# A three-layer relational graph network on one core: gathers without a fill between them, and the first layer's dense pieces planned over its gathers

## The chip, the core and the metric

The kernel runs on one core of a Trainium2 chip. The core has five engines that run side by side, each through its own queue in order, and that meet only at semaphores: TensorE (PE in the profile, its weight loads PEld), VectorE (DVE), ScalarE (ACT), GpSimd (POOL) and SyncE (SP). Sixteen DMA engines move data between HBM and the on-chip memory SBUF; matmuls write into PSUM. What counts is the device time of one execution in microseconds, lower is better.

## What is computed

```python
def _rgcn_conv(x, edge_index, edge_type, W, root, bias):
    src, dst = (edge_index[0], edge_index[1])
    x_src = x[src]
    out = x @ root + bias
    for r in range(N_REL):                       # 4 relations
        mask = (edge_type == r).astype(x.dtype)
        s = segment_sum(x_src * mask[:, None], dst, num_segments=N_NODES)
        c = segment_sum(mask, dst, num_segments=N_NODES)
        mean = s / jnp.maximum(c, 1.0)[:, None]
        out = out + mean @ W[r]
    return out
...
h = x                                            # 6250 x 128, float32
for l in range(2):
    h = relu(_rgcn_conv(h, ..., weights[l], roots[l], biases[l]))
h = _rgcn_conv(h, ..., weights[2], roots[2], biases[2])
return _layernorm(x + h)
```

There are 6250 nodes of 128 features, 100,000 edges sorted by destination and 3 layers. The destinations are drawn as the square of a uniform number, so the first nodes have many incoming edges and the last ones few.

## The kernel before, in words

Edges stand in tiles of 128, 782 of them, and four tiles make a group (196 groups, the last one with two tiles, of which the last has 32 edges). A layer treats them in two ways.

**Sparse groups.** The groups from a certain one on are gathered: the table `ytab` in HBM holds, for each node and relation, the row h @ W[r] (512 bytes), GpSimd issues an indirect DMA for each tile (L734, `gather`) that fetches 128 rows into one quarter of a slot of `ring`, VectorE builds for each tile a 128x128 selection matrix `S` (L1358), and TensorE adds rows times `S` into one of the banks `psGR` and `psRB` (L899), from where VectorE adds a group to the node's columns (`node`, L1380). The first layer gathers 138 groups (550 tiles), the other two 119 groups (474 tiles) each, 1498 tiles in all. The ring has nine slots of four tiles, so GpSimd may be up to 36 tiles ahead of TensorE; then it waits on `s_pe`. Gathers of a layer can start only when the last rows of `ytab` for it have landed.

**Dense windows.** The groups of the first nodes, which have many edges each, are not gathered. They are put together into windows of at most 116 nodes, 5 windows in the first layer and 9 in the others. Of each a count matrix over all 6250 source nodes is built, in 49 blocks: binned records (items "P" and "N": VectorE L1389 to L1393, TensorE L950 and L952), then one-hot matrices on VectorE (L1408, L1409), their product on TensorE (L997), a copy by ScalarE (L1081), and the product with the layer's own rows (L981). A piece of two blocks is a "C" item, 25 pieces a window. Windows built in a layer are kept in HBM (`a_dram`), the next layers load them (`aring`, L1057). The first layer builds windows 0 to 4, the second loads these and builds 5 to 8, the third loads all nine. When a window is whole, the items "M", "F" and "G" scale its sum and multiply it by the weights (L924), the result being added like a group.

**Ends.** As soon as all edges of a block of 128 nodes are in, an "E" item applies the relu and makes the block's rows for the next layer (L775, L780, L781, ScalarE L1010), which SyncE stores to `ytab`. The last layer has "L" items with the layer normalization in their place. The first window's nodes end last, after all dense windows ("late" blocks 0 to 4 in the first layer).

**The order.** All of this stands in one list of items for each layer, and every engine runs its part of that list in order. The list is made by `schedule`, a planner that simulates the layer with costs written out by hand. It assumes that a gather takes `GATHER` = 1.36 us in the first layer and 1.25 us in the others, and it gives each dense item a due time, `due`, that moves by `pace` times the item's cost. A sparse group goes first when the planner believes that it has arrived; a dense item goes in when it is due. With `pace` at 1.0 dense items stand as early as their costs allow; above 1.0 they are spread over the gathers until `ENDING` = 100 us ahead of the last gather:

```python
pace = max(1.0, (sum(ntile) * gather - ENDING) / sum(max(cost(li, it)) for it in dense)) if li else 1.0
```

so that in the first layer it is 1.0 whatever the sums are. The planner's own start times for that layer are `START_POOL` = 95 us and `START_PE` = 205 us.

**The fill.** Behind every gather GpSimd runs `rest` (L724): a memset of 160 int32 on one partition of a tile that nobody reads, `pause`. It waits for the memset before it and nobody else waits for it.

Ahead of all this the kernel turns the input arrays into tiles, makes the first layer's `ytab` (until about 99 us) and counts edges for the scales, on VectorE until about 200 us; the fast path starts on TensorE at 219 us.

Of the kernel before, what the change touches and what calls it, by code (L numbers as in the profile page):

```python
# [8 lines left out]
I32 = mybir.dt.int32  # L9
# [11 lines left out]
NL = 3  # L21
RW = 1024
FAR = 1000000
PAUSE = 160
EPS = 1e-5
WINDOWS = (5, 9, 9)
SPAN = 116
# [2 lines left out]
LAG, ENDING, BEHIND, SPREAD, TURN = 12.0, 100.0, 20.0, 10.0, 6.0  # L30
# [79 lines left out]
def schedule(pl, R):  # L110
# [11 lines left out]
    def cost(li, it):  # L122

        if it[0] == "X":
            return 0.0, 0.7, 0.7
        if it[0] == "P":
            c = pl.win[it[1]][2]
            return 4 * (0.12 + c * 0.04), 1.1 + 4 * (0.07 + 2 * c * pl.NB / 960), 0.0
        if it[0] == "C":
            c, m = pl.win[it[1]][2], len(pl.pieces[it[2]])  # L130
            if it[1] in pl.built[li]:
                return m * (0.44 + 0.22 * c), 0.44 * m * c, 1.0 * m
            return m * 0.44, 0.0, 0.4 * m
        return {"N": (0.0, 2.0, 0.0), "M": (0.5, 0.0, 0.6), "F": (0.0, 0.7, 0.0), "G": (0.9, 0.6, 0.0)}[it[0]]

    for li in range(NL):
        W, KH, sparse = pl.W[li], pl.KH[li], pl.sparse[li]
        NS = len(sparse)
        ntile = [min(4, pl.NT - 4 * g) for g in sparse]
        gather = GATHER[li > 0]  # L140
        start = START_PE if li == 0 else 0.0
        pe = dve = act = start
        pool = START_POOL if li == 0 else 0.0
        arrive, eaten, items = [], [], []
        dense = []
# [22 lines left out]
                        dense.append(("N", w + 1))  # L168
            dense.append(("F", w))
        dense.append(("G", W - 1))  # L170
        pace = max(1.0, (sum(ntile) * gather - ENDING) / sum(max(cost(li, it)) for it in dense)) if li else 1.0
        due = start
        done, late = KH, list(range(KH))
        batch, batches, added = [], [], [0, 0]
# [99 lines left out]
def rgcn_kernel(nc, x, src, dst, typ, weights, roots, biases, c_ident, c_iota, c_tri, c_col, c_need,  # L274
# [30 lines left out]
    rows_of = [min(P, E - t * P) for t in range(NT)]  # L305
    width = [c * NB for _, _, c in pl.win]
    layers = schedule(pl, R)


# [73 lines left out]
    with ctx:  # L383
        sb = lambda name, shape, dt=F32: ctx.enter_context(nc.sbuf_tensor(name, shape, dt))
# [26 lines left out]
        flagf = sb("flagf", [1, 2])  # L411
        brow = sb("brow", [1, 2, NP], I32)
        idxc = sb("idxc", [P, NT4], I32)
        pause = sb("pause", [1, PAUSE], I32)
        relc, wc = sb("relc", [P, NT4]), sb("wc", [P, NT4])
        vals = sb("vals", [P, TH, 2], F16)
        colc = sb("colc", [P, TH])
# [66 lines left out]
        rest = room + NB * P - (2 * NB * P + AF * PIECE * NR * P + AS * CH * NR * P // 2)  # L484
        if rest > 0:
# [9 lines left out]
        tbank = lambda u: (psT + psY)[u % TB]  # L495
        banks_of = lambda li, w: psC[pl.second[li][w]]

        names = ("s_e0 s_e1 s_e2 s_k0 s_k1 s_c s_x0 s_x1 s_w0 s_w1 s_fill s_rest s_idx s_dst s_tot s_prod s_end s_car s_aw s_vio "
                 "s_tp s_tev s_fl s_small s_sm s_st s_xt s_pb s_pu "
                 "s_ym s_rm s_yev s_rev s_tA s_tV s_S s_pe s_acc s_fin s_sq s_sd s_no s_v2 s_v3 "  # L500
                 "s_bd s_oh s_dn s_fd s_fp s_bc s_mb s_xa s_cv tSP tPE tACT tDVE tPOOL gd gp s_xw s_n1").split()
        q = {n: sem(n) for n in names}
# [213 lines left out]
            ring_need[n] = ring_total[n % R]  # L716
        AHEAD = min(R, sbase[1])

        rests = [0]

        def rest(e):
            if rests[0]:
                e.wait_ge(q["s_rest"], rests[0])
            e.memset(pause[:], 0).then_inc(q["s_rest"], 1)  # L724
            rests[0] += 1

        def gather(e, n):
            li, g = sgroups[n]
            if n >= R:
                e.wait_ge(q["s_pe"], n - R + 1)  # L730
            for i, t in enumerate(tiles[g]):
                m = rows_of[t]
                at = (n % R) * 512 + i * P
                e.indirect_dma_start(ring[0:m, at:at + P], None, Y[li % 2],  # L734
                                     bass.IndirectOffsetOnAxis(ap=idxc[0:m, t:t + 1], axis=0)
                                     ).then_inc(s_ring[n % R], 16)
                rest(e)

        def gpsimd_engine(e):
            tail = FULL // 32 * 32  # L740
            e.memset(U[tail:NP, 0:RW].bitcast(I32), 0)
            e.memset(U[tail:NP, RX:RX + RW].bitcast(I32), 0)
            last = e.memset(a_dstx[tail:NP, :], FAR)
            if tail:
                last = e.memset(a_dstx[0:1, 0:1], -1)
            last.then_inc(q["s_fill"], 1)
            e.wait_ge(q["s_tev"], 1)
            y_stored(e, 0)
            for n in range(AHEAD):
                gather(e, n)  # L750
            branch(e, "POOL", pool_fast)

        def pool_fast(e):
            for n in range(AHEAD, NN):
                if n in sbase:
                    y_stored(e, sgroups[n][0])
                gather(e, n)
# [951 lines left out]
```

## Time and profile before

| | us |
|---|---|
| median of 3 runs | 2343.55 |
| lowest, highest | 2343.26, 2344.71 |
| the profiled execution | 2337.83 |
| its span in the trace | 2335.9 |

The span of the trace is 1.9 us shorter than the profiled execution's own time, and that is 5.7 us below the median of the runs. The profile names engines as above; a line number is a line of the kernel before. "Busy" is time in which an instruction of the engine runs, an idle time is put down to what ended it, and "issue" means that nothing in the trace explains it. PEclk is the clock that TensorE was granted, as a share of full speed. Where several forms or buffers share a line they are one group.

In the profiled execution the first layer's gathers start at 99.5 us, the second's at 1000.1 us, the third's at about 1668 us, and the last gather at 2314.5 us.

### The profile page before, as it was taken

The numbers are of one execution on the slowest core, as the hardware profiler recorded it, in microseconds if no ns is written. First come the engines' busy times: TensorE is split into PE (matmuls) and PEld (weight loads), VectorE is DVE, ScalarE is ACT, GpSimd is POOL, SyncE is SP. The second block draws the span as 40 slices with busy tenths as digits, with TensorE's granted clock in tenths as the row PEclk, the third lists the DMA queues.
The fourth block names the chain that finished last, engine by engine and source line by source line (L and its number), as shares of the span: only waits on it lengthen the run. The fifth ranks groups of instructions, "written<-read, shape, count | busy, mean of one in ns | idle before, by whom it ended". The sixth has DMA issues, their size and how long they took to land.

```text
span 2335.9 us, 29108 instructions
## 1 busy us (share of the span) xinstructions
PE 1622.7 (69%) x7831; PEld 1152.8 (49%) x7831; DVE 1249.9 (54%) x4096; ACT 1003.1 (43%) x1499; POOL 1893.7 (81%) x3004
## 2 busy tenths in 40 slices
PE   6513667878998854559898778776577677777643
PEld 4312334545665543347675545544355566665532
DVE  4988889988887522223277665552133233333342
ACT  4300002455788710156666556662344444444200
POOL 0293998888888888678888888888488888888885
PEclk9756667999999965779999899997689888888855
DMA  6300222333444432377654344444455555555321
GB/s 202 125 27 23 60 63 86 106 106 124 140 166 160 167 106 66 95 229 218 218 180 146 124 133 139 139 155 128 148 187 154 165 177 168 170 176 173 106 82 47
DMA packets 164859, 314.38 MB, mean 135 GB/s; under 512 B 34816, under 2 KB 85120, under 8 KB 164692
## 3 DMA queue, kind: packets, MB, share of 16 engines
q1 hardware_dynamic: 113096, 210.74, 26.3%
q0 software_dynamic: 47936, 98.12, 14.9%
q10 hardware_dynamic: 3660, 3.60, 0.6%
q8 instruction: 67, 1.10, 0.2%
q14 instruction: 100, 0.82, 0.1%
HBM read 206.52 MB, written 105.80 MB: 134 GB/s over the span
## 4 chain that ended last, share of the span: by engine, by line
POOL 65%; issue 11%; PE 9%; DVE 8%; DMA 4%; ACT 1%; ACTq 1%; DVEq 0%; SPq 0%; POOLq 0%
POOL ring L734 52%; POOL pause L724 13%; DMA aring<-a_dram 3%; PE psD L981 2%; PE psY L775 2%; ACT afull L1057 1%; DVE rows L1208 1%; PE psRB L899 1%; DVE V L1409 1%; DMA ring<-ytab,idxc 1%; DVE V L1408 1%; ACTq L1027 1%; PE psT L775 1%; DVE S L1358 1%; PE psRB L781 0%
## 5 line engine op out<-in xcount | busy, mean ns | idle before, releaser
L734 POOL DMA_INDIRECT ring<-ytab,idxc x1498 | 1526.5, 1019 | 421.2 <-issue 241.4
L981 PE MATMUL psD<-afull,xs 128*128 128x512 f32 (+1 forms) x1666 | 579.4, 476 | 60.7 <-ACT afull L1057 33.2
L1358 DVE TENSOR_SCALAR S<-iota,relc,wc 128x128 f32<-128x128 f32 x1498 | 426.9, 371 | 161.9 <-PE psGR L899 91.4
L1057 ACT ACTIVATE afull<-aring 128x1024 fp32r<-128x1024 f16 (+1 forms) x350 | 346.7, 1033 | 240.4 <-DMA aring<-a_dram 133.0
L899 PE MATMUL psRB<-S,ring 128*128 128x128 f32 x1516 | 254.7, 321 | 228.1 <-DMA ring<-ytab,idxc 220.0
L899 PE MATMUL psGR<-S,ring 128*128 128x128 f32 x1480 | 249.8, 323 | 219.2 <-DMA ring<-ytab,idxc 208.0
L981 PEld LDWEIGHTS psD<-afull,xs 128*128 128x128 f32 (+1 forms) x1666 | 336.0, 209 | 133.5 <-issue 32.5
L724 POOL MEMSET pause<- 1x160 int32 x1498 | 370.1, 247 | 0.1
L899 PEld LDWEIGHTS psRB<-S,ring 128*128 128x128 f32 x1516 | 227.2, 226 | 269.5 <-issue 210.7
L899 PEld LDWEIGHTS psGR<-S,ring 128*128 128x128 f32 x1480 | 225.5, 229 | 258.0 <-issue 210.2
L1085 ACT ACTIVATE aring<-afull 128x1024 f16<-128x1024 f32 (+1 forms) x225 | 234.0, 1040 | 21.0 <-ACT afull L1081 0.7
L1408 DVE TENSOR_SCALAR V<-iota,recs 128x128 f16<-128x128 f16 x588 | 163.8, 279 | 121.6 <-PE psT L997 73.6
L1081 ACT ACTIVATE afull<-psT 128x512 fp32r<-128x512 f32 x299 | 173.8, 593 | 123.5 <-PE psT L997 121.2
L1409 DVE TENSOR_SCALAR V<-iota,recs 128x512 f16<-128x512 f16 x588 | 212.3, 361 | 0.0
L981 PE MATMUL psB<-afull,xs 128*128 128x512 f32 (+1 forms) x588 | 167.1, 431 | 6.2 <-ACT afull L1057 6.0
L997 PE MATMUL psT<-V 128*128 128x512 f16 x394 | 146.2, 408 | 6.0 <-DVE V L1409 5.7
L1380 DVE TENSOR_TENSOR node<-node,psRB 128x128 f32 x199 | 57.3, 288 | 161.6 <-issue 75.3
L1064 ACT ACTIVATE xs<-xst 128x512 fp32r<-128x512 f32 (+1 forms) x39 | 23.2, 595 | 271.2 <-DMA xst<-in_x 248.8
L981 PEld LDWEIGHTS psB<-afull,xs 128*128 128x128 f32 (+1 forms) x588 | 115.0, 206 | 33.5 <-ACT afull L1057 8.6
L1380 DVE TENSOR_TENSOR node<-node,psGR 128x128 f32 x200 | 57.6, 288 | 135.0 <-DVE node L1380 64.7
L1010 ACT ACTIVATE yst<-psT 128x512 f32<-128x512 f32 (+1 forms) x62 | 36.8, 594 | 213.3 <-PE psT L775 213.3
L1081 ACT ACTIVATE afull<-psY 128x512 fp32r<-128x512 f32 x142 | 84.1, 592 | 70.4 <-PE psY L997 69.8
(198 smaller groups left out, 1569.4 us busy)
## 6 DMA issues: line engine op xcount, KB each, us to landing
aring<-a_dram SPq DMA_DIRECT2D x168, 512.0 KB
a_dram<-aring SPq DMA_DIRECT2D x108, 512.0 KB
ytab<-yst SPq DMA_DIRECT2D x144, 256.0 KB
ring<-ytab,idxc POOLq DMA_INDIRECT x1498
hrows<-yst SPq DMA_DIRECT2D x96, 64.0 KB
xst<-hrows SPq DMA_DIRECT2D x24, 256.0 KB
xst<-in_x SPq DMA_DIRECT2D x12, 256.0 KB
yst<-in_x SPq DMA_DIRECT2D x11, 256.0 KB, 4.3
```

Of the source, the lines that this page charges most:

```text
L724: e.memset(pause[:], 0).then_inc(q["s_rest"], 1)
L734: e.indirect_dma_start(ring[0:m, at:at + P], None, Y[li % 2], bass.IndirectOffsetOnAxis(ap=idxc[0:m, t:t + 1], axis=0)).then_inc(s_ring[n ...
L899: last = e.matmul(o, ring[0:m, at:at + P], S[0:m, n % NS, i, :], start=(i == 0), stop=(i == len(tiles[g]) - 1))
L981: last = e.matmul(bank[:], xs[0:m, s, i, :], a, start=(i == 0 and s == 0), stop=(i == NB - 1 and s == 1))
L997: e.matmul(tbank(u)[:], ohs[:, v % NO, :], ohk[:, v % NO, :], start=(j == 0), stop=(j == c - 1)).then_inc(q["s_bd"], 1)
L1057: e.activation(afull[:, n % AF, 0:m, :], aring[:, cc % AS, o:o + m, :], ACT.Copy).then_inc(q["s_cv"], 1)
L1081: e.activation(afull[:, n % AF, j, :], tbank(u)[:], ACT.Copy).then_inc(q["s_tA"], 1)
L1085: e.activation(aring[:, cc % AS, half:half + m, :], afull[:, n % AF, 0:m, :], ACT.Copy).then_inc(q["s_cv"], 1)
L1358: last = e.tensor_scalar(S[:, n % NS, i, :], iota[:], relc[:, t:t + 1], wc[:, t:t + 1], ALU.is_equal, ALU.mult)
L1380: e.tensor_tensor(w, w, part[bank][:, j * P:(j + 1) * P], ALU.add).then_inc(q["s_acc"], 1)
L1408: e.tensor_scalar(ohs[:, v % NO, :], iota16[:, 0:P], recs[:, 0, at:at + 1], None, ALU.is_equal)
L1409: e.tensor_scalar(ohk[:, v % NO, :], iota16[:], recs[:, 1, at:at + 1], None, ALU.is_equal).then_inc(q["s_oh"], 1)
```

## The change

It has two parts. The fill behind every gather goes, with its tile, its constant and its semaphore. And `pace` is worked out for the first layer as for the others, from the time between the planner's start of the dense work and its last gather: for that layer it becomes (95 + 550 x 1.36 - 205 - 100) / 420.2 = 538 / 420.2 = 1.28, with 420.2 us the sum of its dense costs. For the other layers `pool` and `start` are zero, the value is what it was, and their lists of items are the same item for item. `GATHER` is left as it is.

```diff
-PAUSE = 160
...
-        pace = max(1.0, (sum(ntile) * gather - ENDING) / sum(max(cost(li, it)) for it in dense)) if li else 1.0
+        pace = max(1.0, (pool + sum(ntile) * gather - start - ENDING) / sum(max(cost(li, it)) for it in dense))
...
-        pause = sb("pause", [1, PAUSE], I32)
...
-        rests = [0]
-
-        def rest(e):
-            if rests[0]:
-                e.wait_ge(q["s_rest"], rests[0])
-            e.memset(pause[:], 0).then_inc(q["s_rest"], 1)
-            rests[0] += 1
-
         def gather(e, n):
...
                                      ).then_inc(s_ring[n % R], 16)
-                rest(e)
```

On GpSimd, where the fast path begins (behind the branch on `flag_i`), before:

```order
L706 TENSOR_LOAD flag_i
L706 ISA x2
L707 COMPARE_AND_BRANCH
L734 DMA ring<-ytab,idxc 128x128
L724 MEMSET pause 1x160
L734 DMA ring<-ytab,idxc 128x128
L724 MEMSET pause 1x160
```

and after, with all the rest of the three layers' gathers:

```order
L704 TENSOR_LOAD flag_i
L704 ISA x2
L705 COMPARE_AND_BRANCH
L724 DMA ring<-ytab,idxc 128x128 x513
L724 DMA ring<-ytab,idxc 32x128
L724 DMA ring<-ytab,idxc 128x128 x473
L724 DMA ring<-ytab,idxc 32x128
```

A gather is now followed at once by the next one; nothing else stands between them but, at each fourth, the wait on `s_pe` for a free slot.

On TensorE, at the end of the first layer's last dense window (`psD<-afull,xs` is the product of a block, `psRB<-V,wt` the window's "G", `x4` of `S,ring` one group, and `psT` or `psY<-wt,node` the first of the three matmuls of an "E"), before:

```order
L899 MATMUL psGR<-S,ring 128x128 x4
L997 MATMUL psY<-V 128x512
L981 MATMUL psD<-afull,xs 128x512 x2
L997 MATMUL psT<-V 128x512
L981 MATMUL psD<-afull,xs 128x512 x2
L997 MATMUL psT<-V 128x512
L981 MATMUL psD<-afull,xs 128x512 x6
L924 MATMUL psRB<-V,wt 128x128 x4
L775 MATMUL psY<-wt,node 128x512
L780 MATMUL psY<-ident,node 128x128
L781 MATMUL psY<-node,rt 128x128
L899 MATMUL psRB<-S,ring 128x128 x12
```

and after:

```order
L986 MATMUL psT<-V 128x512
L970 MATMUL psD<-afull,xs 128x512 x2
L888 MATMUL psRB<-S,ring 128x128 x4
L986 MATMUL psY<-V 128x512
L970 MATMUL psD<-afull,xs 128x512 x6
L913 MATMUL psRB<-V,wt 128x128 x4
L888 MATMUL psRB<-S,ring 128x128 x8
L888 MATMUL psGR<-S,ring 128x128 x8
```

The rows look alike, but they stand at another place among the groups: the last dense piece stands behind 104 of the 138 groups before and behind 113 after. Up to the 52nd group the two lists are the same; from there on the dense items move back little by little, by 9 groups at the end. The blocks 0 to 4 ("late") move from behind the 109th group to behind the 117th, and the other ends from the 111th group on keep about the place that they had.

## Rows read from the trace of the kernel before

**Rows 1.** The page: the chain that ended last, shares of the span.

```profile
POOL 65%; issue 11%; PE 9%; DVE 8%; DMA 4%; ACT 1%; ACTq 1%; DVEq 0%; SPq 0%; POOLq 0%
```

**Rows 2.** GpSimd's groups: line, engine, operation, xcount | busy us, mean ns | idle before.

```profile
L734 POOL DMA_INDIRECT ring<-ytab,idxc x1498 | 1526.5, 1019 | 421.2 <-issue 241.4 <-DMA ytab<-yst 95.9 <-DMA hrows<-yst 45.4
L724 POOL MEMSET pause<- 1x160 int32 x1498 | 370.1, 247 | 0.1
```

**Rows 3.** Timeline of GpSimd: start us, us, engine line operation [idle before].

```profile
979.86 0.22 POOL L724 MEMSET pause<- 1x160 int32 x1
1000.11 0.96 POOL L734 DMA_INDIRECT ring<-ytab,idxc  x1 [20.03 <-DMA hrows<-yst]
...
120.54 0.66 POOL L724 MEMSET pause<- 1x160 int32 x1
121.36 1.99 POOL L734 DMA_INDIRECT ring<-ytab,idxc  x1 [0.16 <-issue]
```

**Rows 4.** Busy us (x) by stretch: PE, PEld, DVE, ACT, POOL, then clock, DMA, GB/s.

```profile
219.00:400.00 181.00, 127.58 (x572) 77.03 (x572) 158.78 (x449) 22.85 (x38) 161.68 (x212) 0.70 0.23 67
400.00:800.00 400.00, 349.08 (x1773) 225.10 (x1774) 334.12 (x1283) 268.11 (x413) 355.36 (x550) 0.94 0.41 138
800.00:1000.00 200.00, 103.98 (x427) 74.52 (x426) 52.55 (x199) 32.51 (x85) 158.44 (x268) 0.68 0.32 98
1000.00:1200.00 200.00, 169.09 (x855) 132.76 (x856) 70.69 (x226) 130.55 (x148) 176.07 (x295) 0.95 0.70 221
1200.00:1668.00 468.00, 348.78 (x1714) 234.14 (x1712) 256.73 (x967) 261.76 (x443) 398.34 (x654) 0.90 0.40 134
1668.00:2336.00 668.00, 435.91 (x2023) 354.70 (x2023) 214.27 (x786) 237.62 (x262) 561.99 (x948) 0.79 0.48 149
```

**Rows 5.** By stretch, the fills (L724) alone: busy us (x), clock, DMA, GB/s.

```profile
400.00:800.00 400.00, 77.28 (x275) 0.94 0.41 138
800.00:1000.00 200.00, 31.20 (x134) 0.68 0.32 98
...
1200.00:1668.00 468.00, 82.12 (x327) 0.90 0.40 134
1668.00:2336.00 668.00, 110.50 (x474) 0.79 0.48 149
```

**Rows 6.** TensorE's waits (us, times, longest), in 400:800, 800:1000, 1200:1668, 1668:2336.

```profile
PE psGR L899 <- DMA ring<-ytab,idxc: 6.5, 3, 3.1
PE psRB L899 <- DMA ring<-ytab,idxc: 2.6, 5, 0.9
...
PE psRB L899 <- DMA ring<-ytab,idxc: 43.8, 15, 4.4
PE psGR L899 <- DMA ring<-ytab,idxc: 39.0, 11, 4.3
...
PE psRB L899 <- DMA ring<-ytab,idxc: 52.9, 30, 4.0
PE psGR L899 <- DMA ring<-ytab,idxc: 52.7, 27, 4.2
...
PE psRB L899 <- DMA ring<-ytab,idxc: 102.8, 44, 4.6
PE psGR L899 <- DMA ring<-ytab,idxc: 91.5, 40, 5.2
```

**Rows 7.** Timeline of TensorE: one group behind the first layer's dense work.

```profile
855.06 2.04 PE L899 MATMUL psRB<-S,ring 128*128 128x128 f32 x8 [3.44 <-DMA ring<-ytab,idxc]
```

**Rows 8.** The chain that ended last: the last gather, from its start to landing.

```profile
2314.46 2.13 DMA ring<-ytab,idxc
```

**Rows 9.** Timeline of GpSimd and VectorE beside each other.

```profile
504.39 0.95 POOL L734 DMA_INDIRECT ring<-ytab,idxc  x1 [0.16 <-issue]
504.57 0.24 DVE L1408 TENSOR_SCALAR V<-iota,recs 128x128 f16<-128x128 f16 x1
504.73 0.34 DVE L1409 TENSOR_SCALAR V<-iota,recs 128x512 f16<-128x512 f16 x1
```

More of the change, by code:

```diff
@@ L496, in rgcn_kernel @@
         banks_of = lambda li, w: psC[pl.second[li][w]]
-        names = ("s_e0 s_e1 s_e2 s_k0 s_k1 s_c s_x0 s_x1 s_w0 s_w1 s_fill s_rest s_idx s_dst s_tot s_prod s_end s_car s_aw s_vio "
+        names = ("s_e0 s_e1 s_e2 s_k0 s_k1 s_c s_x0 s_x1 s_w0 s_w1 s_fill s_idx s_dst s_tot s_prod s_end s_car s_aw s_vio "
                  "s_tp s_tev s_fl s_small s_sm s_st s_xt s_pb s_pu "
```

## The prediction

> **What bounds the kernel now.** Read first the chain that ended last: GpSimd holds 65% of the span and unexplained issue time 11% [rows 1]. Then GpSimd's groups: 1498 gathers of 1019 ns on average and as many fills of 247 ns; of the idle time ahead of gathers 241.4 us is "issue", some 0.16 us each [rows 2]. A quiet cycle is thus 0.95 (gather) + 0.22 (fill) + 0.16 (gap) = 1.33 us. Over a layer it is more, since VectorE holds GpSimd up now and then: 1.41 us a tile in the third layer (668 us for 474), 1.54 in the first from 219 us on (781 us with both ends, 515 tiles).
>
> Then the busy times by stretch [rows 4], beside TensorE's waits for gathers [rows 6]; they show where a faster gather would be felt. From 219 to 400 us VectorE is busy for 158.8 of 181 us. From 400 to 800 TensorE (349 of 400) and VectorE (334) are both near full, and TensorE waits 9 us for gathers. From 800 to 1000 the dense work is over, and TensorE waits 82.8 us. From 1000 to 1200 the second layer loads windows (221 GB/s), and there no wait of TensorE for a gather stands in the view. From 1200 to 1668 these waits are 105.6 us, in the third layer 194.3 us. So gathers bound three stretches of six.
>
> **Part 1, the fill goes: what a cycle becomes.** The trace has no gather that follows directly on another. Lower bound: the span of the gather itself, 0.95 us. Upper bound: 1.33 us, because a gather after 20.03 us of idle takes 0.96 us and the one 0.38 us behind its predecessor takes 0.95, and because the gap behind a fill is 0.16 us even where the fill took 0.66 us [rows 3]. If a gather left hidden work behind it of more than 0.38 us, the short break would show it, and a long fill would shorten the gap. Less than 0.38 us of such work can't be seen. I take 1.11 us, gather and gap without the fill: the gap is always there ahead of a gather and is nearest to a cost of starting one.
>
> The Trainium skill ("Perfetto Trace Analysis", on GpSimd's profiler boundary) says that GpSimd's spans don't compose and that such instructions are to be timed from start to start. What agrees here is only that the sole spacing in the rows is 1.33 us; by that rule 0.95 us is no lower bound, and the saving of a removed fill is anything between nothing and more than its length.
>
> **Where it is felt.** In a stretch the gain is the smaller of what the fills cost there [rows 5] and what TensorE waits [rows 6].
>
> First layer. 219 to 400: 106 fills of 0.247 = 26 us, but VectorE has only 181 - 159 = 22 us to spare: 15. 400 to 800: 77 us of fills against 9 us of waits: 9. The other 68 us are not lost: GpSimd runs ahead until the ring of 36 tiles is full. At the stretch's end it is some 6 ahead now (a landing of 2.13 us [rows 8] and a group of four), so 30 more, worth 30 x 1.11 = 33 us. 800 to 1000: 31 us of fills + 33 of lead = 64 of the 82.8 us of waits. Together 88 us.
>
> Second layer. 1000 to 1200: no waits, no gain, but a fuller ring; VectorE and the loads set the pace there, and GpSimd is ahead already, so I count 25 of its 36 us (147 fills of 0.247). 1200 to 1668: 82 + 25 = 107 us against 105.6 of waits. The two don't meet piece by piece, and I take 90.
>
> Third layer. Fills 110.5 us against 194.3 us of waits, nothing else late: the loads are 149 GB/s where the second layer had 221 with TensorE 169 of 200 us busy. I take 102, since locks that fell on a fill (247 - 220 = 27 ns a tile, 13 us) partly fall on the gather instead.
>
> **Part 2, the first layer's order.** The last dense piece stands behind 104 groups before, behind 113 after. Nothing is added: the same items in another order, with SyncE's stores and VectorE's one-hots along with them. A group costs TensorE 2.04 us [rows 7]. Nine groups, 18 us of TensorE's work, come out of the stretch in which it idles and go into the one in which it is full, and the 36 tiles they hold are then eaten before the gather-bound stretch starts. Without part 1 this is worth nothing: the layer ends with its last gather either way. With part 1 the last stretch has 98 tiles, of which 30 are in the ring: 68 x 1.11 = 75 us of gathers instead of 36 more tiles, 115 us; against the 18 us put ahead that leaves at most 22 us, of which TensorE's own work (200 - 82.8 - 18 = 99 us there, some 25 of it the end of the layer) allows little. The blocks 0 to 4 end behind group 117 of 138, still under cover. I take 7 us; the bounds are 0 and 22.
>
> **Sum.** 88 + 7 + 90 + 102 = 287 us. 2337.8 - 287 = 2051; with the 5.7 us by which the median lies above the profiled execution, about 2056 us. The setup up to 219 us is VectorE's and stays: the 36 fills in it stand ahead of a full ring.
>
> **The rivals.** First, the gap goes too, because a gather is taken up while another runs: 1.00 us a cycle. Another 0.11 x 474 = 52 us in the third layer, where 92 us of waits are left; 8 more in the second, where few are left; 15 in the first. About 1980 us. For it: the fill starts at the gather's end without a gap. Against it: the gap stands ahead of every gather, whatever came before. 12%.
>
> Second, a gather leaves hidden work of 0.2 to 0.35 us, which the fill covered; the cycle is about 1.25 us (the planner's own number for the later layers). Saved are 0.08 a tile against a quiet cycle, some 0.10 with the locks on fills gone: 47 us in each later layer, 50 in the first. 2343.5 - 145 = about 2200 us. Nothing in the rows speaks against it. 20%.
>
> Third, all 0.38 us are dead time and the fill was free: no change, 2343 us. The rows would allow it only if the dead time were just as long as fill and gap; and the new order alone gives nothing. 5%.
>
> Fourth, the slower end: without an instruction between them each gather is held until its predecessor's transfer has moved on. Its landing is 2.13 us behind its start [rows 8], so this could cost anything from 0 to 0.8 us a tile; it decides from a cycle of 1.33 us on. At 1.50 us it costs 0.15 x 948 = 142 us in the later layers and about 15 in the first: 2500 us. Against it: now the next gather starts 1.33 us behind the last, well before that landing, unhindered. 6%.
>
> A fifth one, slower too: gathers in a row shut VectorE out, and the breaks of 0.38 us are where it gets in. Full exclusion would make a layer the sum of both engines' work: in the first layer 545 us of VectorE [rows 4] and about 541 of gathers in 781 us. That sum, 1086, is larger than the stretch, and one-hots start and end inside a gather [rows 9]. So only short parts of a gather exclude. Over the three layers gathers and gaps at 1.11 us for 1462 tiles are 1623 us and VectorE's work 1087 us [rows 4], against some 2050 us in which they are gathered now; it takes an exclusion of 40% of VectorE's time to be slower, and half of it gives +120 us, about 2460. Today's cycle in the first layer, at most 0.2 us a tile above the quiet one with 1.06 us of VectorE beside each, allows 20%. 3%.
>
> The Trainium skill ("SBUF — State Buffer", on the shared port pair) states this rule: either side holds the pair "for the full instruction". The trace doesn't agree (two one-hots of 0.24 and 0.34 us within a gather of 0.95); by the rule, with all 1087 us excluded, the time would be near 3000 us.
>
> **Chances.** The forecast of 2056 us: 54%, for itself between 2000 and 2120. The first rival 12%, second 20%, third 5%, fourth 6%, fifth 3%. The range of 8 in 10 takes in the forecast's own, most of the second rival and half of the first: 1975 to 2240. A measurement of this kernel tells 0.2%, about 5 us, from no change. Faster 0.86, the same 0.05, slower 0.09.
>
> **What would show it.** In the new timeline gathers of 0.95 us start 1.11 us apart: 1.00, 1.25 or 1.33 name the first, second or third rival, longer gathers the fourth, longer one-hots and `S` builds the fifth. Waits of GpSimd on TensorE for a free slot should come up between 600 and 800 us and near 1200 us, and nowhere in the third layer. TensorE's waits for gathers should be some 20 us in the first layer's tail, under 20 in the second layer, near 90 in the third. The layers should be shorter by 95, 90 and 102 us. The forecast is wrong if the spacing is not 1.11 us, or if dense work turns out to be late where gathers were: then the third layer's gain is smaller than 100 us with waits for gathers gone.

## The result, and the profile after

| | median us | runs | kernel before beside it |
|---|---|---|---|
| first comparison | 2217.38 | 4 (2216.14 to 2218.82) | 2343.41 (4 runs) |
| once more, in the last set of runs | 2216.65 | 2 | 2345.52 (3 runs) |

The ratio is 0.9462, 95% interval 0.9445 to 0.9478; the second time 0.9455 (0.9427 to 0.9483). The change takes 126 us off, 5.4%. The forecast was 2056 us, a gain of 287 us, so less than half of the expected gain came; the time is near that of the second rival (2200 us) and inside the range. The profiled execution took 2218.8 us, its span is 2217.0 us. Between the two traces the difference is 118.9 us, since the profiled execution of the kernel before lies 5.7 us below its median and that of the changed kernel 1.4 us above. The chain that ended last (as in [rows 1]) is still GpSimd's first of all:

```profile
POOL 49%; issue 18%; DVE 15%; PE 9%; DMA 5%; ACT 1%; DVEq 1%; ACTq 1%; SPq 0%; POOLq 0%
```

What a gather costs now stands in the timeline of GpSimd (as in [rows 3]: start, us, engine, line, operation, idle before):

```profile
1106.35 0.94 POOL L724 DMA_INDIRECT ring<-ytab,idxc  x1 [0.30 <-issue]
1107.60 0.95 POOL L724 DMA_INDIRECT ring<-ytab,idxc  x1 [0.30 <-issue]
```

and in its group (as in [rows 2]):

```profile
L724 POOL DMA_INDIRECT ring<-ytab,idxc x1498 | 1553.1, 1037 | 639.5 <-issue 449.0 <-DMA ytab<-yst 95.4 <-DMA hrows<-yst 48.5
```

The fill's 0.22 us are gone, but the gap ahead of a gather has grown from 0.16 to 0.30 us: undisturbed gathers start 1.25 us apart (1106.35 and 1107.60), where it was 1.33. That is 0.08 us, not 0.22. "Issue" went from 241.4 to 449.0 us, which eats 208 of the 370 us that the fills had. And the gather itself is 1037 ns on average instead of 1019 (18 ns a tile, 27 us). VectorE is what lengthens both. In the trace of before, of the full-size gathers behind 225 us the 448 beside which VectorE ran nothing took at most 0.96 us, and those beside which it was busy up to 2.57 us; a fill took 221 ns without VectorE beside it and 266 with it. In the changed kernel 431 gathers had no VectorE beside them, again at most 0.96 us. So the time that fills had lost to VectorE (some 37 us in all) falls on the gathers in good part.

The stretches (as in [rows 4]: PE, PEld, DVE, ACT, POOL, then clock, DMA share, GB/s). The layers' gathers now start at 99.0, 964.4 and 1601.7 us, the last one at 2195.4:

```profile
400.00:800.00 400.00, 342.32 (x1741) 223.40 (x1740) 327.88 (x1272) 256.30 (x395) 311.45 (x291) 0.93 0.41 136
800.00:966.00 166.00, 100.02 (x426) 69.31 (x424) 49.17 (x190) 43.33 (x100) 108.36 (x114) 0.72 0.37 118
966.00:1166.00 200.00, 170.87 (x857) 135.22 (x858) 70.38 (x227) 130.99 (x148) 152.43 (x157) 0.95 0.72 225
1166.00:1589.00 423.00, 337.15 (x1699) 228.00 (x1697) 253.48 (x966) 256.98 (x433) 314.24 (x317) 0.91 0.44 143
1589.00:2217.00 628.00, 419.00 (x2038) 339.40 (x2036) 211.95 (x786) 240.28 (x272) 450.42 (x474) 0.83 0.52 160
```

The third layer of the kernel before starts at 1676.7 us, and not at about 1668, which lies in the wait ahead of it. The row in its timeline is

```profile
1676.69 0.96 POOL L734 DMA_INDIRECT ring<-ytab,idxc  x1 [25.41 <-DMA hrows<-yst]
```

The second layer's gathers now start 35.7 us earlier (964.4 for 1000.1), the second layer is 39 us shorter (637 for 677), the third 44 (615 for 659). That is 0.07, 0.08 and 0.09 us for each of the 514, 474 and 474 tiles: gathers still set the pace in all three. TensorE's waits for them (as in [rows 6]) say so too; in 800:966, 1166:1589 and 1589:2217:

```profile
PE psRB L888 <- DMA ring<-ytab,idxc: 26.4, 11, 3.8
PE psGR L888 <- DMA ring<-ytab,idxc: 25.0, 8, 3.8
...
PE psGR L888 <- DMA ring<-ytab,idxc: 38.2, 26, 3.7
PE psRB L888 <- DMA ring<-ytab,idxc: 37.9, 25, 3.7
...
PE psRB L888 <- DMA ring<-ytab,idxc: 84.8, 45, 3.5
PE psGR L888 <- DMA ring<-ytab,idxc: 75.9, 41, 4.8
```

51 us where it was 82.8, 76 where it was 105.6, 161 where it was 194.3. GpSimd waited for a free slot only at the start, as before (the longest in each row of `psGR` below is that one; the others are within the 0.30 us that stand ahead of every gather), so the ring was never full later. The first row is of the kernel before:

```profile
POOL ring L734 <- PE psGR L899: 37.6, 3, 37.3
...
POOL ring L724 <- issue: 449.0, 1473, 0.3
POOL ring L724 <- PE psGR L888: 42.5, 8, 40.3
POOL ring L724 <- PE psRB L888: 4.3, 14, 0.3
```

### The profile page after: what moved, and what is told of

It is laid out like the page before. It is cut to its first block, busy times and chain, and to the rows that moved or that the text cites. A ratio compares the mean times of both kernels' runs of the same rounds, so it can differ in the third digit from the quotient of the medians.

```text
span 2217.0 us, 27610 instructions
## 1 busy us (share of the span) xinstructions
PE 1591.0 (72%) x7831; PEld 1130.9 (51%) x7831; DVE 1239.0 (56%) x4096; ACT 1002.8 (45%) x1499; POOL 1556.1 (70%) x1506
## 4 chain that ended last, share of the span: by engine, by line
POOL 49%; issue 18%; DVE 15%; PE 9%; DMA 5%; ACT 1%; DVEq 1%; ACTq 1%; SPq 0%; POOLq 0%
POOL ring L724 49%; DMA aring<-a_dram 2%; PE psY L764 2%; DVE V L1398 2%; DVE S L1347 2%; DMA ring<-ytab,idxc 2%; DVE V L1397 2%; DVE V L1382 1%; PE psD L970 1%; DVE rows L1197 1%; PE psT L764 1%; PE psRB L888 1%; DVEq L1355 1%; ACT afull L1046 1%; DVE node L1369 1%
## 5 line engine op out<-in xcount | busy, mean ns | idle before, releaser
L724 POOL DMA_INDIRECT ring<-ytab,idxc x1498 | 1553.1, 1037 | 639.5 <-issue 449.0
L970 PE MATMUL psD<-afull,xs 128*128 128x512 f32 (+1 forms) x1666 | 572.8, 472 | 59.6 <-ACT afull L1046 33.1
L1347 DVE TENSOR_SCALAR S<-iota,relc,wc 128x128 f32<-128x128 f32 x1498 | 418.4, 365 | 114.5 <-PE psGR L888 74.3
L888 PE MATMUL psRB<-S,ring 128*128 128x128 f32 x1516 | 246.3, 313 | 178.6 <-DMA ring<-ytab,idxc 171.4
L888 PE MATMUL psGR<-S,ring 128*128 128x128 f32 x1480 | 241.6, 316 | 175.5 <-DMA ring<-ytab,idxc 158.1
L888 PEld LDWEIGHTS psRB<-S,ring 128*128 128x128 f32 x1516 | 220.7, 220 | 219.2 <-issue 178.0
L888 PEld LDWEIGHTS psGR<-S,ring 128*128 128x128 f32 x1480 | 218.6, 223 | 213.7 <-issue 167.8
L970 PE MATMUL psB<-afull,xs 128*128 128x512 f32 (+1 forms) x588 | 159.2, 416 | 6.0 <-ACT afull L1046 6.0
L999 ACT ACTIVATE yst<-psT 128x512 f32<-128x512 f32 x66 | 39.2, 595 | 185.0 <-PE psT L764 184.9
L764 PE MATMUL psY<-wt,node 128*128 128x512 f32 (+1 forms) x162 | 94.9, 671 | 22.4 <-DVE node L1487 14.1
```

Source lines behind the costliest of these rows:

```text
L764: e.matmul(y_bank(li, k)[0:bw[k], :], h, wt[:, li].rearrange("i r o -> i (r o)"), start=True, stop=True).then_inc(q["s_ym"], 1)
L888: last = e.matmul(o, ring[0:m, at:at + P], S[0:m, n % NS, i, :], start=(i == 0), stop=(i == len(tiles[g]) - 1))
L970: last = e.matmul(bank[:], xs[0:m, s, i, :], a, start=(i == 0 and s == 0), stop=(i == NB - 1 and s == 1))
L1347: last = e.tensor_scalar(S[:, n % NS, i, :], iota[:], relc[:, t:t + 1], wc[:, t:t + 1], ALU.is_equal, ALU.mult)
```

## Where the 0.30 us come from: fills of four sizes

The spacing between gathers is what the prediction had wrong, so it came first. The kernels differ from the changed one by the old `rest` behind each gather and its size, and each keeps the new order:

```diff
+PAUSE = 1        # 240 and 320 in the others
...
+                rest(e)
```

> The changed kernel (its order, its plan) with a fill of one element (PAUSE = 1) behind every gather, with the semaphore that the kernel before had. In the changed kernel a gather takes 0.94 us and the next starts 0.30 us later, 1.25 us from start to start; in the kernel before the gap behind a fill was 0.16 us. Theory A (hidden work: the 0.30 us is what a gather leaves behind it, whatever follows): the fill lies inside it, the cycle stays 1.25 us, total 2217 us. Theory B (the 0.30 us is the cost of starting a gather behind another gather, and behind a memset it is 0.16 us): the cycle is 0.95 + 0.09 + 0.16 = 1.20 us, 0.05 us less in some 1400 gathers that set the pace, total about 2155 us. If the semaphore's update costs a fixed time, the cycle would be above 1.25 us.

> The changed kernel's order with a fill of 320 elements and its semaphore. The fill is 0.13 us longer than that of 160 (0.22 us). Both theories: nothing hides it, the cycle is 0.95 + 0.35 + 0.16 = 1.46 us, 0.13 us more than in the kernel before, in some 1400 gathers: total near 2343 + 0.13 x 1400 = 2525 us. If the first layer's dense work hides part of it, about 2500 us.

> The changed kernel's order with a fill of 240 elements: 0.95 + 0.29 + 0.16 = 1.40 us from gather to gather. Theory G (the hold-ups of TensorE come when gathers follow closer than some distance between 1.33 and 1.46 us; at 1.46 there were none): few hold-ups, and the time that gathers at 1.40 us give, 2343 + 0.07 x 1400 = about 2440 us, on a chip where the kernel before takes 2490 to 2530 us. Theory H (they come with the chip and the moment whatever the spacing, and the run with 320 elements was lucky): hold-ups as in the others, 2520 us or more.

The timelines of GpSimd, with 1, 240 and 320 elements:

```profile
1062.09 0.09 POOL L724 MEMSET pause<- 1x1 int32 x1
1062.39 0.94 POOL L734 DMA_INDIRECT ring<-ytab,idxc  x1 [0.22 <-issue]
```

```profile
1100.17 0.29 POOL L724 MEMSET pause<- 1x240 int32 x1
1100.62 0.95 POOL L734 DMA_INDIRECT ring<-ytab,idxc  x1 [0.16 <-issue]
```

```profile
1100.97 0.35 POOL L724 MEMSET pause<- 1x320 int32 x1
1101.48 0.95 POOL L734 DMA_INDIRECT ring<-ytab,idxc  x1 [0.16 <-issue]
```

| fill | fill us | gap behind it | from a gather's end to the next one's start | spacing |
|---|---|---|---|---|
| none | - | - | 0.30 | 1.25 |
| 1 element | 0.09 | 0.22 | 0.30 | 1.25 |
| 160 (before) | 0.22 | 0.16 | 0.38 | 1.33 |
| 240 | 0.29 | 0.16 | 0.45 | 1.40 |
| 320 | 0.35 | 0.16 | 0.51 | 1.46 |

So a gather starts 0.16 us behind a fill, and not earlier than 0.30 us behind the last gather. The fill of one element tells the two theories apart: were 0.30 us the price of starting a gather behind a gather, the gap behind the short fill would have been 0.16 and the spacing 1.20 (theory B). It was 0.22, and the sum stayed at 0.30 within rounding (theory A). Something of 0.30 us follows a gather. A fill of up to some 0.14 us should thus cost no spacing; that is an estimate (0.30 less the 0.16 behind a fill), of which the fill of 0.09 us is the only one that was run. What the 0.30 us are inside GpSimd no trace tells, and theory A's time of 2217 us for one element was never met: all three of its runs fell on chips where the engines stop now and then (below), so the spacing alone decides between A and B.

The times follow the spacing. On the chip of the last set, the kernel before at 2345.5 us:

| spacing, order | median us | ratio to before |
|---|---|---|
| 1.25, new (the changed kernel) | 2216.7 | 0.9455 (0.9427 to 0.9483) |
| 1.40, new | 2420.3 | 1.0323 (1.0292 to 1.0355) |
| 1.46, new | 2506.9 | 1.0693 (1.0659 to 1.0727) |

The fills of 240 and 320 elements were expected at about 2440 and 2525 us (2500 with part of it hidden); they took 2420.3 us, and 2509.8 and 2506.9. From 1.249 to 1.396 us (the most frequent spacing in the two traces) the time grows by 203.6 us, or 1385 us for each microsecond of spacing; there are 1462 tiles behind the first ring. So in this range a shorter cycle is felt nearly in full, at 0.95 of the tiles. The forecast had counted somewhat less, 280 us of 1462 x 0.22 = 322. Below 1.25 us no run tells how much would be felt.

## Four chips on which the kernel before takes 2500 us

There are six sets of runs. In the first and the last the kernel before took 2343 and 2346 us, in the four between them, on four different chips, 2494, 2529, 2532 and 2500 us (medians), with another profile. There the change is not worth 5%.

> The changed kernel once more, beside the three others. Where the kernel before takes 2343 us this takes 2217. Where it takes 2490 to 2530 us, as in the last two sets, theory C (in those sets the engines are held up together for a time that no step of the kernel sets, and a faster gather buys nothing there): about as long as the kernel before, within 1%. Theory D (the hold-ups come on top of the kernel's own time): 5% less than the kernel before, as in its first run.

Measured, the changed kernel took 2527.9 us (8 runs) beside 2531.5 (27 runs): ratio 0.9983, interval 0.9942 to 1.0024, no difference that can be told. Theory D falls, C agrees. The kernel before once more, for its trace:

> The kernel before once more, for its profile beside the other runs of this set. In the set before this one (fills of 1 element, of 160 with the new order, none with the old order) the same kernel before took 2476 to 2503 us where it had taken 2343, and the three variants 2483 to 2515, with TensorE, VectorE and ScalarE held up at the same time in places that the profile puts down to nothing or to an unknown queue. If that belongs to the chip or the moment, this run gives either 2343 us without such waits or about 2490 with them; if it belonged to the kernels, this run would be free of it in both cases.

It took 2514.9 us (one run), with the hold-ups, so they belong to the chip or the moment, not to the variants. The chain that ended last, first of this run and then of the changed kernel in the set of c1:

```profile
PE 42%; issue 17%; DVE 13%; another core or an unknown queue 12%; POOL 6%; ACT 4%; DMA 3%; DVEq 1%; ACTq 1%; SPq 0%; POOLq 0%
```

```profile
PE 44%; issue 18%; DVE 15%; another core or an unknown queue 12%; ACT 6%; DMA 2%; DVEq 1%; ACTq 1%; SPq 0%
```

GpSimd had 65% in [rows 1] and has 6% here, or none. What a hold-up looks like is seen in the timeline of the kernel before there: TensorE's weight loads within one group of eight matmuls that wait for nothing between them, and then the first instructions of VectorE and ScalarE behind it ("remote" is a semaphore whose sender the trace does not tell):

```profile
401.20 1.40 PEld L899 LDWEIGHTS psGR<-S,ring 128*128 128x128 f32 x5
403.89 0.29 PEld L899 LDWEIGHTS psGR<-S,ring 128*128 128x128 f32 x1 [1.29 <-issue]
405.99 0.29 PEld L899 LDWEIGHTS psGR<-S,ring 128*128 128x128 f32 x1 [1.81 <-issue]
407.41 0.29 PEld L899 LDWEIGHTS psGR<-S,ring 128*128 128x128 f32 x1 [1.13 <-issue]
429.56 0.50 PEld L775 LDWEIGHTS psT<-wt,node 128*128 128x128 f32 x2 [21.86 <-DVE node L1498]
...
426.50 0.25 DVE L1408 TENSOR_SCALAR V<-iota,recs 128x128 f16<-128x128 f16 x1 [24.14 <-remote]
426.56 0.60 ACT L1081 ACTIVATE afull<-psT 128x512 fp32r<-128x512 f32 x1 [25.22 <-remote]
```

A group that takes 2.04 us in [rows 7] takes over 6 us here. Then TensorE's weight loads stand for 21.86 us, but they stand for VectorE, and VectorE and ScalarE stand too, for 24.14 and 25.22 us: between 409 and 426.5 us none of the three works, while GpSimd goes on with its gathers.

From 219 us on, gaps of 0.9 to 2.5 us between TensorE's matmuls of one group, with no wait in the program, number 58 in this trace and 64 in that of the changed kernel in the set of c1, and there are none in the traces of the first and last sets. Which of the engines is held and which only waits for it can't be read, because the traces of the four sets lack semaphore records: 14,774 updates stand in this one where the trace of [rows 1] has 40,701, and 13,422 for 39,230 with the changed kernel. "Remote" and the share of an unknown queue may be nothing but the missing records. The spans and times do not hang on them.

GpSimd's own spacing is the same as on the other chips (1.33 and 1.25 us where nothing holds it), but it has to wait for slots, 151 us in all behind the first ring in this trace and 297 in that of the changed kernel, where their traces of the first set show none. For the changed kernel (the longest wait on `psGR` is again that behind the first ring):

```profile
POOL ring L724 <- issue: 416.8, 1348, 3.2
POOL ring L724 <- remote: 205.3, 91, 6.4
POOL ring L724 <- PE psGR L888: 103.3, 26, 41.6
```

**Is TensorE the bound there?** One kernel leaves half of the gathers out, and thereby part of the sum, all else in place:

```diff
-            ring_total[n % R] += 16 * len(tiles[g])
+            ring_total[n % R] += 16 * (len(tiles[g]) if n < R else min(2, len(tiles[g])))
...
             for i, t in enumerate(tiles[g]):
+                if n >= R and i >= 2:
+                    continue
```

> The changed kernel with half of the gathers: from the tenth group on only the first two tiles of a group are fetched, TensorE multiplies all four (the others hold older rows), so part of the sum is left out and nothing of the other engines' work. Theory E (where the kernel before takes 2490 to 2530 us TensorE is the bound, held up on its own queue): within 2% of the kernel before there. Theory F (gathers still set the pace in part): 5% or more below it. On a chip where the kernel before takes 2343 us the changed kernel has about 330 us of waits of TensorE for gathers from 219 us on, and this run gives 2217 - 330 = about 1890 us, the time that the other engines need.

It took 1876.8 us (2 runs) beside 2499.6, ratio 0.7503 (0.7430 to 0.7577). Its output is wrong, as half of the rows are old ones; its time counts. Theory E falls: TensorE can do all of its work in 1877 us on such a chip. The number is within theory F's, but this kernel also has none of the hold-ups (one such gap between matmuls, of 0.95 us, where the kernels with the hold-ups have 43 to 82), so it doesn't tell that the gathers' spacing set the pace there. The chain now is the other engines' own work:

```profile
DVE 32%; PE 27%; issue 14%; DMA 13%; ACT 8%; DVEq 3%; another core or an unknown queue 1%; ACTq 1%; SPq 1%
```

The unknown queue has 1% where the kernels with all gathers at 1.25 or 1.33 us have 8 to 16. So the hold-ups come with the full number of gathers. All matmuls are still in it. The time is also near what is left of the changed kernel's 2217 us without TensorE's waits for gathers (171.4 + 158.1 = 330 us over the whole span): 1887 us.

**Does it hang on the spacing?** The run with 320 elements in the first of these sets took 2509.8 us (one run) beside a kernel before of 2493.5 us, and its chain reads as in the first and last sets:

```profile
POOL 68%; issue 11%; DVE 8%; PE 6%; DMA 4%; ACT 1%; ACTq 1%; DVEq 0%; SPq 0%; POOLq 0%
```

> The fill of 320 elements again, 1.46 us from gather to gather. Theory G: 2510 us within 0.5%, as at its first run, whatever the kernel before takes. Theory H: 2580 us or more, hold-ups on top of its own time.

In the last set, where the kernel before takes 2346 us, it took 2506.9 us. So the same kernel lost nothing on a chip on which the kernel before loses 150 us. That, and half of the gathers, agree with theory G, that the hold-ups come when gathers are closely spaced for long. But on a chip with hold-ups it is one run; the last set, with 240 and 320 elements, had no hold-ups and so decides nothing between G and H. One more rival is open: fewer gathers in the same time also mean fewer events to record, and every time here is that of a recorded execution. In the run with 320 elements on a chip of the four, too, some records are missing (27,979 updates for 40,803 in the last set), without a hold-up. Whether the hold-ups come from the gathers, or from the recording of so many events, and why on these chips, no run here shows.

The other runs on these chips, the fill of one element, the new order alone and the missing fill alone:

> The changed kernel with a fill of one element behind every gather, again. The trace of its first run shows the start-to-start spacing of undisturbed gathers at 1.245 to 1.25 us, as without a fill: theory A (hidden work of 0.30 us behind a gather) holds there, theory B (1.20 us) does not. In an undisturbed run theory A gives 2217 us, equal to the changed kernel within 5 us; theory B 2155 us.

> The changed kernel with a fill of one element behind every gather. Hidden work of 0.30 us behind a gather (theory A): spacing 1.25 us as without a fill, the same time as the changed kernel within 0.3%. Starting cost (theory B): spacing 1.20 us, 2.5% less.

| kernel | three sets, ratio to before with interval |
|---|---|
| fill of 1 element, new order | 1.0084 (1.0054 to 1.0114), 1.0048 (1.0017 to 1.0079), 1.0048 (1.0015 to 1.0081) |
| no fill, old order | 1.0081 (1.0046 to 1.0116), 1.0050 (1.0023 to 1.0076), 1.0025 (0.9994 to 1.0055) |
| fill of 160, new order | 0.9977 (0.9946 to 1.0008), 0.9966 (0.9937 to 0.9996), 0.9951 (0.9912 to 0.9990) |
| the change (both parts) | 0.9983 (0.9942 to 1.0024), third set only |

There, taking the fill out costs 0.3 to 0.8%, the new order gains 0.2 to 0.5%, and together they come to nothing. One interval of three takes in no change in each of these two rows, and none of the kernels is 2% away from the kernel before. In the third set a fill of one element is 0.7% slower than no fill (2546.7 and 2527.9 us) though their spacing is the same; why is open.

## The two parts apart

Each part alone:

```diff
 # new order alone: the kernel before with
-        pace = max(1.0, (sum(ntile) * gather - ENDING) / sum(max(cost(li, it)) for it in dense)) if li else 1.0
+        pace = max(1.0, (pool + sum(ntile) * gather - start - ENDING) / sum(max(cost(li, it)) for it in dense))
...
 # no fill alone: the changed kernel with these two lines the other way round
```

> The kernel before with the second part of the change alone: the fill of 160 elements stays, the first layer's dense pieces are planned over its gathers. Theory (the new order alone gives nothing, since the first layer ends with its last gather): 2343 us, the second layer's gathers start at 1000 us as before. Rival (the spread dense work and VectorE's locks on GpSimd are also spread, and gathers in the first layer get through sooner or later): up to 15 us either way.

> The changed kernel with the first part alone: no fill, the first layer's dense pieces as early as before. Theory (the first layer is bound by its gathers at 1.25 us with or without the new order): 2217 to 2222 us. Rival (the new order is worth the 7 us that the prediction gave it, or the up to 22 us that were its bound): 2224 to 2240 us, with the second layer's gathers starting that much later than 964 us.

> The kernel before with the new order alone, again. Undisturbed: 2343 us if the order is worth nothing while the gathers set the pace; 2330 us if it spreads VectorE's holds on GpSimd; ratio to the kernel before 1.000 or 0.995.

> No fill, the old order, again. Undisturbed: 2217 to 2222 us if the first part of the change is all of the gain; 2224 to 2240 us if the order takes the 7 to 22 us of the prediction.

> The fill of 160 elements with the new order. Ratio to the kernel before 1.000 if the order is worth nothing under gathers that set the pace, 0.995 at the most.

> No fill with the old order. In undisturbed runs 2217 to 2222 us if part 1 is all of the gain, 2224 to 2240 us if part 2 has the 7 to 22 us that the prediction allowed it.

> Fill and new order. Where gathers set the pace: 2343 us if the order alone is worth nothing. Where TensorE is held up: 0.3 to 0.5% below the kernel before, as in the last three sets.

> No fill and old order. Where gathers set the pace: 2217 to 2222 us if part 1 is all of the gain, 2224 to 2240 us if part 2 has 7 to 22 us of it. Where TensorE is held up: 0.3 to 0.8% above the kernel before, as in the last three sets.

All eight ran on chips where the kernel before takes about 2500 us, so none of them tells how 126 us split where gathers set the pace. The last two are single runs, 2479.7 and 2518.0 us beside 2499.6: 0.8% below and 0.7% above. What can be said for that comes from the last set,

> The changed kernel on the same chip, 1.25 us from gather to gather. Theory G: hold-ups, 2510 to 2530 us, within 0.5% of the kernel before, as at its second run. On a chip like the first one 2217 us.

in which three spacings ran with the new order. The second layer's first gather there, with no fill and with 240 elements:

```profile
965.18 0.95 POOL L724 DMA_INDIRECT ring<-ytab,idxc  x1 [22.03 <-DMA hrows<-yst]
```

```profile
1023.92 0.96 POOL L734 DMA_INDIRECT ring<-ytab,idxc  x1 [20.14 <-DMA hrows<-yst]
```

On a straight line between them the kernel before's spacing of 1.33 us gives 998 us, and its old order has 1000.1 us in its trace. By this estimate the new order alone is worth some 2 us in the first layer. By the same line the other two layers, whose order is unchanged, come out 1 and 4 us off in the same direction, so the method can't tell 2 us from nothing. The medians say more: on the line from 2216.7 to 2420.3 us a spacing of 1.33 us gives about 2329 us with the new order, and the kernel before takes 2345.5 us in the same set, 17 us more. Some 8 us of these 17 lie between the median of the kernel before and its profiled execution, and no trace shows where. So part 1 is some 110 to 124 us and part 2 some 2 to 17, both estimates from the line; the 0.2 to 0.5% (6 to 12 us, and 20 us in the single run) that the new order gains on the other chips lie about there. No run has part 2 alone where gathers set the pace.

## Why the prediction was wrong, point by point

**The bound.** Right that gathers set the pace and that their start-to-start spacing was the thing to ask for. But "gathers bound three stretches of six" is too little: behind the first ring GpSimd never waited for a slot, before or after, so each layer ended with its last gathers and their time counted in every stretch. The prediction let most of it in again as a lead in the ring.

**Part 1, the cycle.** This is the step that failed. "I take 1.11 us, gather and gap without the fill: the gap is always there ahead of a gather and is nearest to a cost of starting one". It was 1.25. The prediction had seen that up to 0.38 us behind a gather could not be seen under fill and gap, and still valued it at nothing. The fill stood in the 0.30 us that a gather leaves behind, so removing 0.22 us saved 0.08. The Trainium skill's rule on GpSimd ("Perfetto Trace Analysis", section "GPSIMD Engine Instruction", on the profiler boundary: time such instructions from start to start) was the one to follow; the trace agrees, since the fill's span of 0.22 us was no measure of what its removal gives.

**Where it is felt.** The layers were to be shorter by 95, 90 and 102 us; with 0.08 instead of 0.22 us a tile they were shorter by 36, 39 and 44. The caps of the sum (VectorE's 22 us from 219 to 400, the full ring, 105.6 us of waits) were never reached. So the signs named for them did not come either: no waits of GpSimd for a slot between 600 and 800 us or near 1200, and TensorE's waits for gathers were 51, 76 and 161 us where some 20, under 20 and near 90 were named. The second rival had 50, 47 and 47: its mechanism was right. Its time of 2200 us was 17 us too low; it took the time lost to VectorE on fills as gone, and the gathers became 18 ns longer each (27 us in all), a term it did not have.

**Part 2.** 7 us were forecast with bounds of 0 and 22; by interpolation 2 to 17 came. That neither confirms the 7 nor refutes it. The way it was to act, through a full ring at the end of the dense work, did not happen: the ring was never full. How the order acts, if it does, is open.

**The rivals.** The first (1.00 us), third (no change on such a chip), and fifth (VectorE shut out) did not happen; VectorE's `S` builds take 365 ns each, 371 before. The fourth, gathers held, did not happen at GpSimd. But on four chips the third's outcome came about by something that the prediction did not have, stops of TensorE, VectorE and ScalarE whose cause is open; the trace of before, taken without them, shows nothing of it.

**Slips.** 781 us for 515 tiles are 1.52 us a tile, not 1.54; the third layer starts at 1676.7 us, so it takes 659 us for 474 tiles, 1.39 each and not 1.41; and a cycle of 1.50 us is 0.17 us above 1.33, not 0.15. None of them moves the forecast.

## What to carry to other kernels

A short instruction between two long ones of the same engine may be standing in time that is dead anyway. Where the trace has no pair without it, the saving lies between nothing and the filler with its gap, and the span of the gap behind it is no price of the next instruction. One kernel with the filler at its smallest size decides it (here 0.09 + 0.22 us, within rounding the 0.30 us of no filler). And a gain of 5% that was measured on one chip should be asked for on a second one: here it was 0.2% on another, with an interval that takes in no change.

## What the runs showed of the hardware

- An indirect DMA of 128 rows on GpSimd is followed by 0.30 us in which the next can't start. The spacing is 1.25 us with no memset and with a memset of 0.09 us between them; behind a memset of 0.22, 0.29 or 0.35 us the next gather starts after 0.16 us, so that the spacing is 1.33, 1.40 or 1.46 us.
- VectorE lengthens what GpSimd does beside it: at most 0.96 us for a gather with VectorE idle, up to 2.57 us with it busy, and 221 or 266 ns for the fill. With the fills gone, the gathers went from 1019 to 1037 ns on average.
- In four sets of six, on four chips, the kernel before took 150 to 190 us more, with gaps of 1.1 to 1.8 us between TensorE's matmuls of one group that wait for nothing and with longer stops of three engines together. A kernel with 0.13 us more between gathers took the same on both kinds of chip (2509.8 us in one run, and 2506.9), and one with half of the gathers 1877 us. Why is open.
